# The zero-point column sums of an attention product: made once for the second half and added by VectorE, in place of two small products per tile and half row

## The chip, the cores and the metric

The kernel runs on one core of a Trainium2 chip. Times are device microseconds of one execution. The kernel before takes 328.64 us, the median of three runs (328.39 to 329.71).

## What is computed

The input x is [2, 512, 1024] in f32, so 1024 tokens in two halves (the two batches). Each half has its own context matrix of 1024 x 1024. Cut to what matters:

```
fake_quant(x) = (clip(round(x / s + z), 0, 255) - z) * s
x = x + tanh(g_xattn) * matmul(fake_quant(layernorm(x)), fake_quant(ctx))
h = layernorm(x)
x = x + tanh(g_ffn) * ( sum over 2 of 16 experts of gate * mlp_e(h)  +  mlp_shared(h) )
```

The quantized values are whole numbers. The kernel keeps them as f16 after taking 128 off (q - 128), so the matrix product of the stored values lacks terms in the difference between 128 and the zero point: one that depends on the output's row alone (row sums, `r1`), and one that depends on its column alone, (128 - z1) times the column sum of the stored context. The second is what the change is about.

## The kernel before, in words

Tokens lie in eight tiles of 128 (`NT` = 8), four per half (`TB` = 4). X holds them all in SBUF. The program is written per engine, with semaphores between them; each engine works through its own list in order.

- **Attention product.** For a tile i, `products(i, k)` makes two products of 128x512 for each of eight k (L1083), 16 in all, into two PSUM banks given by `AT_BANK` (tile 4: banks 0 and 1, tile 5: 2 and 3, tile 6: 4 and 5, tile 7: 6 and 7). `column_sums(i)` (L1086 to L1092) adds four more into the same banks: the stationary C1 holds (128 - z1) in each place, as a high and a low f16 half, and the moving S2 is the sum of the eight context blocks, so that each row of the result gets the scaled column sum. It then signals `at_done`.
- **Attend** (L711, VectorE) reads the two banks, scales them by `cf[:, 4:5]` and adds them to X. Then `bn` (L640 to L643) takes the statistics for the layer norm, GpSimd raises the variance to -0.5 (L373), `coefs` (L650, L651) gives scale and offset, and ScalarE writes the normed rows twice, in f32 and f16 (L433, L437). `ln2_lo` (L720, VectorE) makes the low f16 half, one tile behind. For the second half a DMA transpose on SyncE's queue (L275) then turns the tile.
- **Second half.** VectorE's list is, for i = 4 to 7 (L937 to L943): attend(i), bn(i), ln2_lo(i-1) from i = 5 on, coefs(i); then ln2_lo(7), and after it the four `sd_evac` (L742), and `route`. ScalarE's list is `hi_chunk("sw3", 0..3)` (L426), `ln_rows(4..7)`, then `add_r1` (L448), which signals `x_r1` for each tile, and the exponential of the router.
- **TensorE's list**: the shared up projection of the first half (L1145), row sums (L1103), the loop over tiles 4 to 7 (L1245 to L1256), and then `shared_down(i)` for the first half's tiles, 24 products each (L1184), into banks `SD_BANK` = (0, 2, 4, 0). Tile 0 waits for attend of tile 4, tile 1 for that of tile 5, tile 2 for that of tile 6. Tile 3 uses banks 0 and 1 again and waits for `sd_read` 1 (L1263), VectorE's first `sd_evac`. Behind it stand the router (L1191, L1193), which waits for the transposed tiles, the shared up projection of the second half, and then the experts (L1306, L1327).
- `su_gate` (L725, VectorE) signals `su_hf`; its fourth frees banks 6 and 7, in which the shared up projection had its last chunk. `clamp_ctx` (L677, L681) makes the context blocks and S2, and signals `s2_rdy`. `lo_chunk` is L694, `add_shared_bias` L956, `row_terms` L698.

Of the kernel before, what the change touches and what calls it, by code (L numbers as in the profile page):

```python
# [4 lines left out]
F32, F16, I32, I16 = mybir.dt.float32, mybir.dt.float16, mybir.dt.int32, mybir.dt.int16  # L5
ALU = mybir.AluOpType
ACT = mybir.ActivationFunctionType
AX = mybir.AxisListType.X

P = 128  # L10
B, S, D = 2, 512, 1024
KC = D // P
NT = B * S // P
TB = NT // B
# [3 lines left out]
SC = SI // P  # L18
# [15 lines left out]
def build(nc, x, ctx_in, g_xattn, g_ffn, x1_scale, x1_zp, x2_scale, x2_zp, router_w, router_b, router_bias,  # L34
# [5 lines left out]
    with es:  # L40
        def sb(name, shape, dt):
            return es.enter_context(nc.sbuf_tensor(name, shape, dt))
# [3 lines left out]
        def sem(name):  # L46
            sems[name] = es.enter_context(nc.semaphore(name))
            return sems[name]


        X = sb("X", [P, NT, D], F32)
# [11 lines left out]
        def view(area, lo, n, dt, pat=None, **kw):  # L63
            v = area[:, lo:lo + n]
            if dt is not F32:
                v = v.bitcast(dt)
            return v.rearrange(pat, **kw) if pat else v

        XT = view(areaT, 0, 8192, F16, "p (h k t) -> p h k t", h=2, k=KC)
        Q2 = view(area2, 0, 4096, F16, "p (k n) -> p k n", k=KC)  # L70
        Q1T = view(areaQ, 0, 2048, F16, "p (j k t) -> p j k t", j=TB, k=KC)
# [13 lines left out]
        S2 = sb("S2", [P, D], F16)  # L85
# [2 lines left out]
        ebr = sb("ebr", [E, SI], F32)  # L88
        EBT = sb("EBT", [P, 2 * HC, E], F32)
        GTE = sb("GTE", [P, NT, E], F32)  # L90
        gcol = sb("gcol", [P, 2, NT], F32)
        gcb = sb("gcb", [P, 2, NT], F32)
        ecol = sb("ecol", [P, 2, 2 * HC], F32)
# [7 lines left out]
        cf = sb("cf", [P, 16], F32)  # L101
# [10 lines left out]
        onesh = sb("onesh", [P, P], F16)  # L112
# [5 lines left out]
        PS = es.enter_context(nc.psum_tensor("PS", [P, 8, 512], F32))  # L118
# [31 lines left out]
        AT_BANK = (0, 4, 6, 2, 0, 2, 4, 6)  # L150
# [19 lines left out]
        c_int, q2_rdy, s2_rdy, c1_rdy = sem("c_int"), sem("q2_rdy"), sem("s2_rdy"), sem("c1_rdy")  # L170
# [3 lines left out]
        sbr_in, sb_T, sbT_rdy = sem("sbr_in"), sem("sb_T"), sem("sbT_rdy")  # L174
        r1_done = sem("r1_done")
        at_done, at_read = sem("at_done"), sem("at_read")
        ln_xs, ln_hi, ln_lo = sem("ln_xs"), sem("ln_hi"), sem("ln_lo")
        tk_T, tk_hi, tk_lo = sem("tk_T"), sem("tk_hi"), sem("tk_lo")
        rw_hi, rw_lo, sb3_in, b3_in, x_add = sem("rw_hi"), sem("rw_lo"), sem("sb3_in"), [sem("b3_in0"), sem("b3_in1")], sem("x_add")
        eb_in, eb_T, ebt_rdy = sem("eb_in"), sem("eb_T"), sem("ebt_rdy")  # L180
        su_done, su_silu, su_hf, su_hi, su_lo = sem("su_done"), sem("su_silu"), sem("su_hf"), sem("su_hi"), sem("su_lo")
# [20 lines left out]
        def arrived(eng, r):  # L202

            eng.wait_ge(ring_in[r % 4], 16 * (r // 4 + 1))
# [19 lines left out]
        def expert_count(eng):  # L224
            return eng.value_load(nact[0:1, 0:1], min_val=MIN_EXPERTS, max_val=E)
# [162 lines left out]
        def _(act):  # L388
# [30 lines left out]
            def hi_chunk(kind, k):  # L419
                r = RING_AT[kind, 0, k]  # L420
                arrived(act, r)
                if kind == "sw":
                    dst = SW[:, 0, k, :, :].rearrange("p k n -> p (k n)")
                else:
                    dst = SW3[:, 0, k, :]
                nc.scalar.activation(dst, ring[:, r % 4, :], ACT.Copy, scale=WS).then_inc(sw_hi, 1)  # L426

            def ln_rows(i):

                act.wait_ge(coef2, i + 1)  # L430
                if i >= 2:
                    act.wait_ge(ln_lo, i - 1)
                nc.scalar.activation(rows[:, i % 2, :], X[:, i, :], ACT.Identity, bias=lnB[:, i:i + 1],  # L433
                                     scale=lnA[:, i:i + 1]).then_inc(ln_xs, 1)
                if i >= TB + 2:
                    act.wait_ge(sw_lo, SW3_LO + SC)
                nc.scalar.activation(WROW[i][:, 0:D], X[:, i, :], ACT.Identity, bias=lnB[:, i:i + 1],  # L437
                                     scale=lnA[:, i:i + 1]).then_inc(ln_hi, 1)
# [78 lines left out]
            su_hi_of(3)  # L517
            hi_chunk("sw3", 2)
            hi_chunk("sw3", 3)
            for i in range(TB, NT):  # L520
                ln_rows(i)
            add_r1(0)
# [7 lines left out]
            def columns(a, j):  # L530

                e = expert_of(act, a)
                if not (isinstance(a, int) and a < 2):
                    act.wait_ge(y_rdy, NV * a - NV)
                    act.sem_inc(waited, 1)
                nc.scalar.activation(gcol[:, j, :], GTE[:, :, bass.ds(e, 1)].rearrange("p t o -> p (t o)"), ACT.Copy)\
                    .then_inc(cols_rdy, 1)
                nc.scalar.activation(gcb[:, j, :], GTE[:, :, bass.ds(e, 1)].rearrange("p t o -> p (t o)"), ACT.Copy,
                                     scale=DNS).then_inc(cols_rdy, 1)
# [60 lines left out]
            n = expert_count(act)  # L600
# [25 lines left out]
        def _(dve):  # L626
            chain = [0]

            def link(ins):

                chain[0] += 1
                ins.then_inc(v_chain, 1)
                dve.wait_ge(v_chain, chain[0])

            v = nc.vector
            norms = [0]

            def bn(i):
                for h in range(2):
                    ins = v.bn_stats(stats[:, i, 6 * h:6 * h + 6], X[:, i, h * 512:(h + 1) * 512])  # L640
                link(ins)
                link(v.bn_aggr(mv[:, i, :], stats[:, i, :]))
                v.tensor_scalar(lnV[:, i:i + 1], mv[:, i, 1:2], EPS, None, ALU.add).then_inc(mv_rdy, 1)  # L643
# [43 lines left out]
            def lo_chunk(kind, k):  # L687
                r = RING_AT[kind, 0, k]
                dve.wait_ge(sw_hi, (k if kind == "sw" else 2 * SC + k) + 1)
                if kind == "sw":  # L690
                    lo, hi = (SW[:, h, k, :, :].rearrange("p k n -> p (k n)") for h in (1, 0))
                else:
                    lo, hi = SW3[:, 1, k, :], SW3[:, 0, k, :]
                v.scalar_tensor_tensor(lo, ring[:, r % 4, :], WS, hi, ALU.mult, ALU.subtract).then_inc(sw_lo, 1)  # L694

            def row_terms(b):
                dve.wait_ge(r1_done, b + 1)
                v.tensor_scalar(r1[:, b * TB:(b + 1) * TB], PS[:, 3, 0:TB], cf[:, 7:8], cf[:, 6:7], ALU.mult, ALU.add)\  # L698
                    .then_inc(r1_rdy, 1)
# [7 lines left out]
            def attend(i):  # L707

                dve.wait_ge(at_done, i + 1)
                pb = AT_BANK[i]  # L710
                v.scalar_tensor_tensor(X[:, i, :].rearrange("p (h n) -> p h n", h=2), PS[:, pb:pb + 2, :], cf[:, 4:5],  # L711
                                       X[:, i, :].rearrange("p (h n) -> p h n", h=2), ALU.mult, ALU.add)\
                    .then_inc(at_read, 1)
                dve.wait_ge(at_read, i + 1)
# [57 lines left out]
            def route():  # L772
# [33 lines left out]
                link(v.tensor_tensor(t2, sco, t1, ALU.mult))  # L806
                v.tensor_scalar(GTE[:, :, :], t2, cf[:, 11:12], None, ALU.mult).then_inc(gte_rdy, 1)

# [61 lines left out]
            clamp_ctx(0, 6)  # L870
            link(v.tensor_scalar(cf[:, 9:10], sc6[:, 3:4], -1.0, HALF, ALU.mult, ALU.add))
            link(v.tensor_scalar(cf[:, 7:8], cf[:, 4:5], cf[:, 9:10], None, ALU.mult))
            link(v.tensor_scalar(cf[:, 6:7], cf[:, 7:8], cf[:, 8:9], float(D), ALU.mult, ALU.mult))
            row_terms(0)
            shared_biases()
# [58 lines left out]
            su_low(3)  # L934
            for c in range(1, SC):
                lo_chunk("sw3", c)
            for i in range(TB, NT):  # L937
                attend(i)
                bn(i)
                if i > TB:  # L940
                    ln2_lo(i - 1)
                coefs(i, 1, None, XS, None)
# [85 lines left out]
            n = expert_count(dve)  # L1028
# [35 lines left out]
        def _(pe):  # L1064
            mm = nc.tensor.matmul
# [14 lines left out]

            def products(i, k):
                for h in range(2):
                    mm(PS[:, AT_BANK[i] + h, :], Q1T[:, i % TB, k, :], Q2[:, k, h * 512:(h + 1) * 512],  # L1083
                       start=(k == 0), stop=False)

            def column_sums(i):  # L1086

                for h in range(2):
                    for n in range(2):
                        last = mm(PS[:, AT_BANK[i] + h, :], C1[:, n, :], S2[:, h * 512:(h + 1) * 512], start=False,  # L1090
                                  stop=(n == 1))
                last.then_inc(at_done, 1)  # L1092
# [112 lines left out]
            for k in range(2):  # L1205
                products(1, k)
# [34 lines left out]
            expert_bias_columns()  # L1241
            row_sums(1)
            pe.wait_ge(q2_rdy, 2 * KC)
            pe.wait_ge(s2_rdy, 2)
            for i in range(TB, NT):  # L1245
                if i == TB:
                    pe.wait_ge(tk_hi, TB)
                    pe.wait_ge(tk_lo, TB)
                if i == TB + 1:
                    pe.wait_ge(r1_rdy, B)  # L1250
                    pe.wait_ge(ebt_rdy, 2)
                if i >= TB + 2:
                    pe.wait_ge(su_hf, i - TB + 1)
                for k in range(KC):
                    products(i, k)
                column_sums(i)  # L1256

            pe.wait_ge(sw_lo, SW3_LO + SC)
            for i in range(TB):
# [31 lines left out]
            n = expert_count(pe)  # L1291
# [83 lines left out]
```

## Time and profile before

| | us |
|---|---|
| median of three runs | 328.64 |
| profiled execution, its own time | 328.81 |
| its span, first to last instruction | 327.0 |
| TensorE busy | 301.6 (92%) |
| VectorE busy | 196.6 (60%) |
| ScalarE busy | 113.6 (35%) |
| GpSimd busy | 15.1 (5%) |

In the profile PE is TensorE's matmuls, PEld its weight loads, DVE is VectorE, ACT is ScalarE, POOL is GpSimd and SP is SyncE. The chain is followed back from the last instruction, at each step to what released it. A timeline row can merge neighbours of one kind; a start that lies before the end of the row above is a pipelined instruction. What is idle before an instruction and who ended it stands in brackets behind it. Row ends of matmuls are modelled, so the distance between starts is the better measure.

### The profile page before, as it was taken

What the parts mean: (1) busy time and instruction counts of PE and PEld (TensorE: products, weight loads), DVE (VectorE), ACT (ScalarE), POOL (GpSimd) and SP (SyncE); (2) the same over time, 40 slices, a digit from 0 to 9 for tenths busy, and PEclk for the clock granted to TensorE, in tenths of its full rate; (3) what the DMA queues carried; (4) which work ended last, traced back from release to release, by engine and by line L of the source; (5) the groups of instructions that cost most, each with busy time, mean ns of one, the idle gap of its engine ahead of it and who ended that gap; (6) DMA issues with size and microseconds to landing.
All of it is one profiled execution on the core that took longest, in us unless ns stands there. A gap on an engine that the chain in (4) does not pass through costs nothing.

```text
span 327.0 us, 4761 instructions
## 1 busy us (share of the span) xinstructions
PE 301.6 (92%) x1895; PEld 153.7 (47%) x1895; DVE 196.6 (60%) x334; ACT 113.6 (35%) x128; POOL 15.1 (5%) x25
## 2 busy tenths in 40 slices
PE   0389879989999999999999999999999999999992
PEld 0234379964454444644444444444444444444441
DVE  3876995786698864585754445448744407125543
ACT  2887257867682369100113600127010001110000
POOL 2100210020000310000000000000000000000000
PEclk9999979999999999999999999999999999999998
DMA  7999044129980363000840003900000000000355
GB/s 268 416 317 299 1 130 130 43 95 222 310 299 1 69 125 64 2 2 0 274 176 3 0 0 112 335 4 2 0 1 0 2 0 0 3 0 0 129 206 186
DMA packets 32775, 34.56 MB, mean 106 GB/s; under 512 B 14788, under 2 KB 27116, under 8 KB 32748
## 3 DMA queue, kind: packets, MB, share of 16 engines
q1 hardware_dynamic: 32736, 34.20, 33.1%
q8 instruction: 17, 0.28, 0.4%
q14 instruction: 10, 0.08, 0.1%
q10 hardware_dynamic: 12, 0.00, 0.0%
HBM read 26.86 MB, written 4.19 MB: 95 GB/s over the span
## 4 chain that ended last, share of the span: by engine, by line
PE 82%; SPq 7%; DVE 5%; ACT 1%; DMA 1%; issue 1%; POOL 1%; DVEq 0%
PE PS L1306 25%; PE PS L1145 19%; PE PS L1327 13%; PE PS L1184 13%; PE PS L1083 5%; SPq L244 4%; PE PS L1161 3%; DVE stats L640 2%; SPq L236 1%; PE PS L1090 1%; DMA sbr<-in_L_ffn_sb_dram 1%; DVE X L711 1%; PE PS L1191 1%; DVE areaW L694 1%; PE PS L1169 1%
## 5 line engine op out<-in xcount | busy, mean ns | idle before, releaser
L1145 PE MATMUL PS<-areaT,areaW 128*128 128x512 f16 x288 | 62.6, 379 | 1.4 <-DVE SA L725 1.4
L1145 PEld LDWEIGHTS PS<-areaT,areaW 128*128 128x128 f16 x288 | 28.0, 98 | 35.0 <-DVE SA L725 1.6
L1184 PE MATMUL PS<-SW,areaH 128*128 128x512 f16 x192 | 41.8, 379 | 0.0
L1327 PE MATMUL PS<-areaW,areaH 128*128 128x512 f16 x192 | 41.8, 379 | 0.0
L1306 PE MATMUL PS<-areaT,area 128*128 128x512 f16 x192 | 41.6, 379 | 0.0
L1306 PE MATMUL PS<-areaT,areaW 128*128 128x512 f16 x192 | 41.6, 379 | 0.0
L584 ACT ACTIVATE SA<-PS,ecol 128x512 f32<-128x512 f32 x8 | 5.5, 687 | 93.2 <-PE PS L1306 93.2
L1083 PE MATMUL PS<-area,areaQ 128*128 128x512 f16 x128 | 31.2, 395 | 0.2
L1021 DVE SCALAR_TENSOR_TENSOR X<-PS,gcol,X 128x1024 f32<-128x1024 f32 (+1 forms) x18 | 21.0, 1164 | 15.8 <-PE PS L1327 15.8
L1327 PEld LDWEIGHTS PS<-areaW,areaH 128*128 128x128 f16 x192 | 18.8, 98 | 22.6
L1306 PEld LDWEIGHTS PS<-areaT,area 128*128 128x128 f16 x192 | 18.8, 98 | 22.7
L1306 PEld LDWEIGHTS PS<-areaT,areaW 128*128 128x128 f16 x192 | 18.8, 98 | 22.7
L1184 PEld LDWEIGHTS PS<-SW,areaH 128*128 128x128 f16 x192 | 18.8, 98 | 22.7
L992 DVE SCALAR_TENSOR_TENSOR SA<-PS,ecol,SA 128x512 f32<-128x512 f32 x8 | 6.0, 751 | 38.2 <-ACT SA L584 38.2
L640 DVE BATCH_NORM_STATS2 stats<-X 128x6 f32<-128x512 f32 x32 | 20.5, 682 | 4.3 <-DMA X<-in_x_dram 4.1
L1083 PEld LDWEIGHTS PS<-area,areaQ 128*128 128x128 f16 x128 | 12.4, 101 | 15.4 <-DVE area L677 1.3
L1009 DVE SCALAR_TENSOR_TENSOR X<-rows,gcb,X 128x1024 f32<-128x1024 f32 x16 | 19.5, 1279 | 0.0
L373 POOL TENSOR_TENSOR lnR<-lnV,mhalf 128x1 f32<-128x1 f32 (+1 forms) x13 | 13.5, 1035 | 102.3 <-DVE lnV L643 102.3
L1161 PE MATMUL PS<-areaT,areaW 128*128 128x128 f16 x256 | 16.6, 230 | 1.2 <-issue 1.2
L462 ACT ACTIVATE SA<-PS,sbT 128x512 f32<-128x512 f32 x8 | 5.5, 683 | 34.3 <-PE PS L1145 32.1
L433 ACT ACTIVATE rows<-X,lnB,lnA 128x1024 f32<-128x1024 f32 x8 | 9.9, 1240 | 20.7 <-DVE lnB L651 20.7
L1161 PEld LDWEIGHTS PS<-areaT,areaW 128*128 128x128 f16 x256 | 16.0, 104 | 1.4 <-issue 1.3
(152 smaller groups left out, 294.9 us busy)
## 6 DMA issues: line engine op xcount, KB each, us to landing
ring<-in_L_ffn_sw_dram SPq DMA_DIRECT2D x12, 512.0 KB, 5.1
X<-in_x_dram SPq DMA_DIRECT2D x8, 512.0 KB, 6.1
areaT<-in_ctx_dram SPq DMA_DIRECT2D x8, 512.0 KB, 10.9
ring<-in_ctx_dram SPq DMA_DIRECT2D x8, 512.0 KB, 3.8
ring<-in_L_ffn_ew_dram SPq DMA_DIRECT2D x4, 1024.0 KB, 7.7
out_dram<-X SPq DMA_DIRECT2D x7, 512.0 KB, 2.7
wrow<-in_L_ffn_ew_dram SPq DMA_DIRECT2D x2, 1024.0 KB, 9.8
rows<-in_L_ffn_eb_dram SPq DMA_DIRECT2D x2, 512.0 KB, 9.8
```

The source lines that it names most:

```text
L244: sp.dma_start(ring[:, r % 4, :].rearrange("p (k n) -> p k n", k=KC), w.rearrange("(k p) n -> p k n", p=P)[:, :, (k // 2) * P:(k // 2 + 1) ...
L373: nc.gpsimd.tensor_tensor(lnR[:, lo:lo + n], lnV[:, lo:lo + n], mhalf[:, 0:n], ALU.pow)\
L433: nc.scalar.activation(rows[:, i % 2, :], X[:, i, :], ACT.Identity, bias=lnB[:, i:i + 1], scale=lnA[:, i:i + 1]).then_inc(ln_xs, 1)
L640: ins = v.bn_stats(stats[:, i, 6 * h:6 * h + 6], X[:, i, h * 512:(h + 1) * 512])
L1009: v.scalar_tensor_tensor(X[:, i, :], rows[:, j, :], gcb[:, j, i:i + 1], X[:, i, :], ALU.mult, ALU.add)\
L1021: v.scalar_tensor_tensor(Xi, PS[:, pb + lo:pb + hi, :], gcol[:, j, i:i + 1], Xi, ALU.mult, ALU.add)\
L1083: mm(PS[:, AT_BANK[i] + h, :], Q1T[:, i % TB, k, :], Q2[:, k, h * 512:(h + 1) * 512], start=(k == 0), stop=False)
L1145: last = mm(PS[:, 4 + 2 * (c % 2) + w, lo:hi], SW[:, wp, 2 * c + w, k, :], XT[:, xp, k, tk], start=(k == 0 and n == 0), stop=(k == KC - 1 ...
L1161: mm(PS[:, 4 + 2 * c + w, tk], SW[:, 0, 2 * c + w, k, :], XT[:, xp, k, tk], start=(k == 0 and xp == 0), stop=False)
L1184: last = mm(PS[:, pb + h, :], HT[:, hp, c, i * P:(i + 1) * P], SW3[:, wp, c, hs], start=(c == 0 and n == 0), stop=(c == SC - 1 and n == 2))
L1306: last = mm(PS[:, 4 + 2 * (u % 2) + w, :], W12S[j][:, wp, w, k, c * P:(c + 1) * P], XT[:, xp, k, tk], start=(k == 0 and n == 0), stop=(k = ...
L1327: last = mm(PS[:, 2 * (i % 2) + h, :], HE[:, hp, c, i * P:(i + 1) * P], W3S[j][:, wp, c, hs], start=(c == 0 and n == 0), stop=(c == HC - 1 ...
```

## The change

For the second half alone, the column sums are made once. After the products of tile 4, TensorE multiplies a matrix of ones with S2, in two products, into banks 6 and 7, which tile 7 uses later (`column_row`, which waits for S2 and for the banks). It signals `cs_done`. ScalarE, after its last sw3 chunk and before its first layer norm row, reads the two banks, scales them by `cf[:, 5:6]` = `cf[:, 4:5]` x (128 - z1), and writes them to a new SBUF tile RC of 128x1024 f32 (`rc_rdy`). VectorE adds RC to each tile's X after attend and before the statistics, in f32 (`add_columns`). The `column_sums` of tiles 4 to 7, 16 products, are gone, and `at_done` comes from the last of the products. TensorE waits for `rc_rdy` before tile 7. The wait for `s2_rdy` 2 moves from ahead of tile 4 to `column_row`. The first half is as it was.

```diff
--- before.py
+++ after.py
@@ -88,6 +88,7 @@
         ebr = sb("ebr", [E, SI], F32)
         EBT = sb("EBT", [P, 2 * HC, E], F32)
         GTE = sb("GTE", [P, NT, E], F32)
+        RC = sb("RC", [P, D], F32)
         gcol = sb("gcol", [P, 2, NT], F32)
         gcb = sb("gcb", [P, 2, NT], F32)
         ecol = sb("ecol", [P, 2, 2 * HC], F32)
@@ -174,6 +175,7 @@
         sbr_in, sb_T, sbT_rdy = sem("sbr_in"), sem("sb_T"), sem("sbT_rdy")
         r1_done = sem("r1_done")
         at_done, at_read = sem("at_done"), sem("at_read")
+        cs_done, rc_rdy = sem("cs_done"), sem("rc_rdy")
         ln_xs, ln_hi, ln_lo = sem("ln_xs"), sem("ln_hi"), sem("ln_lo")
         tk_T, tk_hi, tk_lo = sem("tk_T"), sem("tk_hi"), sem("tk_lo")
         rw_hi, rw_lo, sb3_in, b3_in, x_add = sem("rw_hi"), sem("rw_lo"), sem("sb3_in"), [sem("b3_in0"), sem("b3_in1")], sem("x_add")
@@ -517,6 +519,9 @@
             su_hi_of(3)
             hi_chunk("sw3", 2)
             hi_chunk("sw3", 3)
+            act.wait_ge(cs_done, 1)
+            nc.scalar.activation(RC.rearrange("p (h n) -> p h n", h=2), PS[:, AT_BANK[NT - 1]:AT_BANK[NT - 1] + 2, :],
+                                 ACT.Identity, scale=cf[:, 5:6]).then_inc(rc_rdy, 1)
             for i in range(TB, NT):
                 ln_rows(i)
             add_r1(0)
@@ -870,6 +875,7 @@
             clamp_ctx(0, 6)
             link(v.tensor_scalar(cf[:, 9:10], sc6[:, 3:4], -1.0, HALF, ALU.mult, ALU.add))
             link(v.tensor_scalar(cf[:, 7:8], cf[:, 4:5], cf[:, 9:10], None, ALU.mult))
+            link(v.tensor_scalar(cf[:, 5:6], cf[:, 4:5], cf[:, 8:9], None, ALU.mult))
             link(v.tensor_scalar(cf[:, 6:7], cf[:, 7:8], cf[:, 8:9], float(D), ALU.mult, ALU.mult))
             row_terms(0)
             shared_biases()
@@ -934,8 +940,14 @@
             su_low(3)
             for c in range(1, SC):
                 lo_chunk("sw3", c)
+            def add_columns(i):
+
+                dve.wait_ge(rc_rdy, 1)
+                link(v.tensor_tensor(X[:, i, :], X[:, i, :], RC[:, :], ALU.add))
+
             for i in range(TB, NT):
                 attend(i)
+                add_columns(i)
                 bn(i)
                 if i > TB:
                     ln2_lo(i - 1)
@@ -1080,8 +1092,17 @@
 
             def products(i, k):
                 for h in range(2):
-                    mm(PS[:, AT_BANK[i] + h, :], Q1T[:, i % TB, k, :], Q2[:, k, h * 512:(h + 1) * 512],
-                       start=(k == 0), stop=False)
+                    last = mm(PS[:, AT_BANK[i] + h, :], Q1T[:, i % TB, k, :], Q2[:, k, h * 512:(h + 1) * 512],
+                              start=(k == 0), stop=(i >= TB and k == KC - 1))
+                return last
+
+            def column_row():
+
+                pe.wait_ge(s2_rdy, 2)
+                pe.wait_ge(su_hf, SC)
+                for h in range(2):
+                    last = mm(PS[:, AT_BANK[NT - 1] + h, :], onesh[:, :], S2[:, h * 512:(h + 1) * 512], start=True, stop=True)
+                last.then_inc(cs_done, 1)
 
             def column_sums(i):
 
@@ -1241,7 +1262,6 @@
             expert_bias_columns()
             row_sums(1)
             pe.wait_ge(q2_rdy, 2 * KC)
-            pe.wait_ge(s2_rdy, 2)
             for i in range(TB, NT):
                 if i == TB:
                     pe.wait_ge(tk_hi, TB)
@@ -1251,9 +1271,13 @@
                     pe.wait_ge(ebt_rdy, 2)
                 if i >= TB + 2:
                     pe.wait_ge(su_hf, i - TB + 1)
+                if i == NT - 1:
+                    pe.wait_ge(rc_rdy, 1)
                 for k in range(KC):
-                    products(i, k)
-                column_sums(i)
+                    last = products(i, k)
+                last.then_inc(at_done, 1)
+                if i == TB:
+                    column_row()
 
             pe.wait_ge(sw_lo, SW3_LO + SC)
             for i in range(TB):
```

## Rows read from the trace of the kernel before

**Rows 1.** The page: busy time by engine, and the chain that ended last.

```profile
PE 301.6 (92%) x1895; PEld 153.7 (47%) x1895; DVE 196.6 (60%) x334; ACT 113.6 (35%) x128; POOL 15.1 (5%) x25
...
PE 82%; SPq 7%; DVE 5%; ACT 1%; DMA 1%; issue 1%; POOL 1%; DVEq 0%
```

**Rows 2.** The chain in order of time, 93 to 132 us: start, length, what.

```profile
93.50 3.48 PE PS L1083 x16
96.97 0.86 PE PS L1090 x4
97.84 3.45 PE PS L1083 x16
...
110.79 20.72 PE PS L1184 x96
```

**Rows 3.** The chain in order of time, its last stages.

```profile
300.53 20.73 PE PS L1327 x96
```

**Rows 4.** Busy time by stretch: PE, PEld, DVE, ACT, POOL, granted clock, DMA share.

```profile
93.50:110.79 17.29, 17.29 (x81) 7.83 (x80) 15.82 (x28) 8.27 (x9) 2.05 (x2) 1.00 0.30 96
```

**Rows 5.** Timeline of VectorE, 92 to 125 us: start, length, instruction, idle before.

```profile
92.32 0.69 DVE L681 TENSOR_TENSOR S<-S,area 128x1024 f16<-128x1024 f16 x1
...
94.13 0.74 DVE L725 SCALAR_TENSOR_TENSOR SA<-PS,sbT,SA 128x512 f32<-128x512 f32 x1
...
99.94 1.27 DVE L711 SCALAR_TENSOR_TENSOR X<-PS,cf,X 128x1024 f32<-128x1024 f32 x1
101.24 1.29 DVE L640 BATCH_NORM_STATS2 stats<-X 128x6 f32<-128x512 f32 x2
...
103.90 1.28 DVE L711 SCALAR_TENSOR_TENSOR X<-PS,cf,X 128x1024 f32<-128x1024 f32 x1
...
108.79 1.28 DVE L711 SCALAR_TENSOR_TENSOR X<-PS,cf,X 128x1024 f32<-128x1024 f32 x1
...
113.68 1.28 DVE L711 SCALAR_TENSOR_TENSOR X<-PS,cf,X 128x1024 f32<-128x1024 f32 x1
...
121.16 1.23 DVE L720 TENSOR_TENSOR ring<-rows,ring 128x1024 f16<-128x1024 f32 x1 [2.51 <-ACT ring L437]
122.30 2.47 DVE L742 SCALAR_TENSOR_TENSOR X<-PS,cf,X 128x1024 f32<-128x1024 f32 x2
```

**Rows 6.** Timeline of ScalarE, 96 to 130 us.

```profile
96.86 1.06 ACT L426 ACTIVATE SW<-ring 128x1024 f16<-128x1024 f32 x1 [0.37 <-DMA ring<-in_L_ffn_sw_dram]
104.02 1.24 ACT L433 ACTIVATE rows<-X,lnB,lnA 128x1024 f32<-128x1024 f32 x1 [6.10 <-DVE lnB L651]
...
120.97 8.40 ACT L448 ACTIVATE X<-X,r 128x1024 f32<-128x1024 f32 x8
```

**Rows 7.** Timeline of VectorE around the early coefficients.

```profile
29.80 0.28 DVE L698 TENSOR_SCALAR r<-PS,cf 128x4 f32<-128x4 f32 x1 [1.18 <-PE PS L1103]
```

**Rows 8.** One line's instructions, L956: min, median and max of their ns.

```profile
L956 DVE SCALAR_TENSOR_TENSOR X<-areaQ,cf,X x8: 1279/1279/1281, 158.3 to 172.2; 128x1024 f32<-128x1024 f32 x8
```

**Rows 9.** One line's instructions, L275, on SyncE's queue, and their time to landing.

```profile
L275 SPq DMA_TRANSPOSE areaT<-ring x2: 1530/1738/1946, 117.9 to 122.5; - x2
...
DMA to landing us min/median/max: 4.2/4.3/5.9
```

**Rows 10.** Timeline of TensorE at 40 us, then the chain in order of time.

```profile
40.28 0.62 PE L1127 MATMUL PS<-idh,wrow 128*128 128x128 f16 x8 [1.07 <-ACT wrow L437]
...
43.55 5.36 PE PS L1161 x64
...
51.59 3.62 PE PS L1161 x64
```

**Rows 11.** Busy time by stretch, columns as in group 4.

```profile
44.30:47.70 3.40, 3.40 (x36) 3.40 (x34) 3.33 (x7) 1.41 (x2) 1.48 (x1) 0.51 0.54 159
```

**Rows 12.** Timeline of TensorE, the transposes of the first tiles.

```profile
14.26 1.03 PE L1078 MATMUL PS<-idh,areaQ 128*128 128x128 f16 x8 [2.42 <-DVE areaQ L665]
...
19.41 1.03 PE L1078 MATMUL PS<-idh,areaQ 128*128 128x128 f16 x8 [0.44 <-DVE areaQ L665]
```

## The prediction

> **What bounds the kernel now.** I read first the chain of work that ended last and the busy shares [rows 1]. TensorE is busy 92% of the span and holds 82% of the chain, so this is a TensorE kernel, and the first question is whether it waits anywhere near the change. The chain in order of time [rows 2] shows that it does not: from 93.50 us the pieces on TensorE follow one another without a gap, through the second half's attention, the 96 products of the shared down projection (20.72 us, so 5.18 for each of its four tiles, to 131.51) and on to the router. The stages behind it are chained on TensorE as well, up to the last product of the span at 321.26 [rows 3]. So whatever moves TensorE between 93 and 134 us moves the end by as much, as long as the others keep up.
>
> Then I asked who could fail to keep up. From 93.50 to 110.79 us VectorE is busy 15.82 of 17.29 us [rows 4], nearly as full as TensorE, and the change gives it more. Its queue in order of time [rows 5] shows one repeating unit per token tile: attend (L711), statistics (L640 to L643), a round trip to GpSimd, which the low half of the tile before (L720) nearly fills, and the coefficients. Attend starts at 99.94, 103.90, 108.79 and 113.68 us: a period of 4.89 us, made by VectorE and the round trip, not by the products, which end every 4.31 us [rows 2] and had run ahead. VectorE therefore already falls behind TensorE in this stage. After the fourth tile comes the wait for ScalarE's layer norm rows (2.51 us), then L720, then the first of the two L742 at 122.30, which frees banks 0 and 1 about 123.58. For that TensorE waits by `sd_read` before the fourth tile of the down projection, which it starts at 110.79 + 3 x 5.18 = 126.33. The slack is 126.33 - 123.58 = 2.75 us. This number decides the case.
>
> **The change part by part.** *Removed from TensorE:* 16 column products, 0.86 us for each four [rows 2], 3.44 us. *Added:* two products of the same shape, 2 x 0.215 = 0.43. Net 14 products, 3.01 us less work, all on the chain. The two have new waits. `su_hf` 4 is given by the L725 that starts at 94.13 and takes 0.74; `s2_rdy` 2 by the L681 of 92.32 [rows 5]. Both are past when the products of the first tile end at 96.97, so the waits cost nothing; with a VectorE 2 us later there they would begin to.
>
> *Added to ScalarE:* one Identity of 128x1024 out of PSUM. No row has this form. The nearest are 1.06 us for L426 and 1.24 for L433, both of that size and from SBUF [rows 6]; I take 1.24. ScalarE ends its last sw3 chunk at 97.92 and is then idle 6.10 us [rows 6]; the sums are there by 97.4 (96.97 + 0.43). So the row RC is ready about 99.1 and costs nothing there. Its two readers come later: VectorE at 101.24, TensorE's fourth tile (banks 6 and 7) at 93.50 + 3 x 3.45 + 0.43 = 104.3.
>
> *Added to VectorE, early:* one 128x1 link, an estimate of 0.2 us, just before the 1.18 us of idle time ahead of L698 [rows 7]. It is covered, and would cost its 0.2 us without that cover.
>
> *Added to VectorE, late:* four f32 additions of 128x1024 in SBUF, each between attend and the statistics of its tile, each waited for by the engine itself, with the statistics, GpSimd's power, the coefficients, ScalarE's two rows, the DMA transpose and the next attend queued behind it. The trace has no f32 addition of two f32 tensors. From below: L681 adds f16 tensors of this size in 0.69 us [rows 5]. From above: L956, f32 with a scalar, takes 1.279 [rows 8]. In between, and nearest in kind, L720 with one f32 operand takes 1.225 [rows 5]. I take 1.225, plus 0.03 us for the self-wait as between L711 at 99.94 (1.27 long) and L640 at 101.24: 1.25 us a tile. Nothing in the unit can absorb it: the addition is serial with the round trip, and every wait of the unit lies behind it. Four tiles give 5.0 us. (The Trainium skill, "VectorE: DVE Perf Modes", section "The perf-mode tier table", says that a `tensor_tensor` on fp32 has only the single rate and the doubled rate is for 16-bit; by that rule the four cost 4 x 1.25, by the f16 row 4 x 0.72. No row here shows the form itself.)
>
> *What is late then.* VectorE's start into the stage doesn't move: at 99.94 it comes from L694 work, not from the products. So the first L742 ends at 123.58 + 5.0 = 128.6 us. ScalarE's `x_r1` comes from L448, which follows the last L437 and moves from 120.97 to 126.0, with its first at 127.1 [rows 6]: just in time. TensorE arrives at the fourth tile at 126.33 - 3.01 = 123.3 and stands until 128.6, that is 5.3 us idle. Against 126.33 that is +2.3 us: the whole 3.0 is lost, and 2.3 more. The other waits of the down projection hold: tile 1 needs the second attend (105.2 + 1.25 = 106.4, against 113.0) and tile 2 the third (110.1 + 2.5 = 112.6, against 118.1). The last transposed tile lands about 122.5 + 4.2 + 5.0 = 131.7 [rows 9], and the router starts at 128.6 + 5.2 = 133.8 or later, so it stays hidden, by 2 us.
>
> *The clock.* A stall of this length hasn't happened to a warm TensorE in this trace. The nearest is the stretch from 39.2 to 43.55 us, where the engine, 1.07 us idle before L1127, did only small batches like the eight transposes of 0.62 us [rows 10]. 0.75 us after dense work had resumed, the granted clock fell to the lower level, 1.2 GHz, and stayed there 3.4 us [rows 11]. The 64 products that began at 43.55 took 5.36 us, the same 64 later 3.62 [rows 10]: 1.74 us lost. A stall of 5.3 us without any work should do it at least as surely. From above: at the start the eight transposes took 1.03 us at 14.26 and at 19.41 [rows 12], against 0.62 later [rows 10]. The slow rate thus lasted from 14.26 to about 20.4 (19.41 + 1.03) through mostly busy time, 6 us, of which half, 3.0, is lost. From below: zero. I take 2.1, near the one priced case and a little up, because here the idleness is complete. (The Trainium skill, "TensorE: Matmul & The Clock Gate", section "Part 1: The HAM clock gate", names the same two levels, 1.2 GHz after idleness and 2.4 after sustained work; by that the loss is there, without it the sum ends at +2.3.) No later wait covers this loss, as everything behind is chained on TensorE.
>
> **Sum.** -3.0 (products) + 5.3 (stall) + 2.1 (clock) = +4.4 us. The profiled execution is 328.81 us with a span of 327.0; the median of the runs is 328.64, 0.17 lower. So 333.2 against the profiled run, and 333.0 against the median.
>
> **The rivals.** (a) *Stall, but the clock holds.* For it: no row shows a fall after pure idleness of this length, and a stall that is shorter by a microsecond may pass. Against: less idleness than this was enough at 44 us. Time 328.64 + 2.3 = 330.9. (b) *The addition runs at the f16 rate.* Four times 0.72 is 2.9, so the release comes at 126.5, 0.1 after the old start: 328.8, and with a fallen clock up to 330.5. Against it stands L720, whose one f32 operand was enough for 1.225. (c) *The gain stays, faster.* If VectorE's delay never reached TensorE, because the order of waits left more slack than the profile shows or VectorE caught up, nearly all of the 3.0 would show: with the release still at 123.58 TensorE gains 2.75 us, 325.9. Every microsecond of delay to the first L742 comes straight off this gain, so that it decides from 2.75 us on, or 0.69 us a tile: an addition has to be cheaper than that. (d) *A long slow phase:* the lower clock lasts through the fourth tile and part of the router, 3.0 us or more: 333.9 to 334.6. (e) *The change doesn't do what it says*, with the two new products waiting: possible only if `su_hf` 4 came after 97.0, 2.1 us later than now; it would also give a slower kernel.
>
> **How the numbers follow.** The forecast (stall and a fallen clock, 331.9 to 333.8) has a chance of 0.62, (a) 0.16, (d) 0.08, (b) 0.06, (c) 0.07, (e) 0.01. The range 330.6 to 334.4 holds the forecast, (a) and most of (d). A difference under 0.5%, 1.6 us, can't be told from no change; (a) lies at +0.7%, close to it, so a part of it goes to "same": faster 0.08, same 0.10, slower 0.82.
>
> **What would show it.** In the profile after: 128 products of the shape of L1083 as before, but 2 in place of 16 column products in the second half; TensorE idle about 5.3 us before the fourth tile of the down projection, released by VectorE's evacuation; attend starts about 6.1 us apart instead of 4.89; the new addition x4 at about 1.22 us; a granted clock of 0.5 for some 3 to 5 us around 128 to 134 us. If the addition takes 0.7 us, (b) is true. If TensorE has no idle time there, my reading of the `sd_read` wait is wrong. If the clock stays at 1.00, (a) is true and I am 2 us too high. If ScalarE's row comes after 101.2 us, the delay is larger than my 5.0.

## The result: 1.3 to 1.5% slower

The changed kernel takes 332.88 us (median of six, 331.3 to 334.3), the kernel before 328.29 in the same group. The ratio is 1.0145, with a 95% interval of 1.0115 to 1.0176. A second group of the same two gave 332.83 us and 1.0128 (1.0093 to 1.0163). The prediction was 333.0. Two executions of the kernel with two additions, 331.39 and 814.59 us, count as slow and are left out of its median below.

The slices of the page before, for TensorE and its granted clock (each slice 8.2 us):

```profile
PE   0389879989999999999999999999999999999992
...
PEclk9999979999999999999999999999999999999998
```

The page of the profile after, its busy times and the same slices:

```profile
PE 300.1 (91%) x1881; PEld 151.3 (46%) x1881; DVE 201.6 (61%) x339; ACT 114.7 (35%) x129; POOL 15.1 (5%) x25
...
PE   0389789989999975999999999999999999999994
...
PEclk9999999999999996999999999999999999999998
```

TensorE has 14 matmuls fewer, VectorE 5.0 us more work. There is a hole in TensorE's line at slices 15 and 16, where there was none, and the clock of slice 16 is lower. The slice with a lower clock at 41 to 49 us is gone; that one comes and goes, as is shown below. The timeline of TensorE in this stretch (start, length, instruction, idle before), to be read against [rows 2]:

```profile
91.56 3.61 PE L1095 MATMUL PS<-area,areaQ 128*128 128x512 f16 x16
95.01 0.59 PE L1104 MATMUL PS<-S,onesh 128*128 128x512 f16 x2
95.44 10.52 PE L1095 MATMUL PS<-area,areaQ 128*128 128x512 f16 x48
105.80 15.70 PE L1205 MATMUL PS<-SW,areaH 128*128 128x512 f16 x72
126.96 8.21 PE L1205 MATMUL PS<-SW,areaH 128*128 128x512 f16 x24 [5.45 <-DVE X L747]
```

L1095 are the products that were L1083, L1104 the two new ones, L1205 the down projection that was L1184. The first three tiles of the down projection follow at once, the fourth stands 5.45 us until VectorE's evacuation (L747, before L742), and then takes 8.21 us, in place of the 5.34 that 24 products take in this view at the full clock (the kernel without additions, below). The busy time by stretch shows the same (PE, PEld, DVE, ACT, POOL, granted clock, DMA share, GB/s):

```profile
121.50:126.00 4.50, 0.01 (x1) 0.00 (x0) 1.92 (x4) 4.08 (x4) 0.00 (x1) 1.00 0.62 117
126.00:132.70 6.70, 5.74 (x14) 2.11 (x15) 3.20 (x3) 6.68 (x8) 0.00 (x0) 0.50 0.41 78
132.70:135.00 2.30, 2.30 (x11) 0.97 (x10) 0.00 (x0) 1.20 (x1) 0.00 (x0) 0.98 0.00 0
```

The granted clock is at its lower level, 1.2 GHz (0.50), from 126.0 to 132.7 us, after 4.5 us without work. VectorE's timeline, against [rows 5]:

```profile
98.13 1.28 DVE L716 SCALAR_TENSOR_TENSOR X<-PS,cf,X 128x1024 f32<-128x1024 f32 x1
99.44 1.23 DVE L946 TENSOR_TENSOR X<-X,RC 128x1024 f32<-128x1024 f32 x1
100.71 1.29 DVE L645 BATCH_NORM_STATS2 stats<-X 128x6 f32<-128x512 f32 x2
...
103.36 1.27 DVE L716 SCALAR_TENSOR_TENSOR X<-PS,cf,X 128x1024 f32<-128x1024 f32 x1
...
109.51 1.28 DVE L716 SCALAR_TENSOR_TENSOR X<-PS,cf,X 128x1024 f32<-128x1024 f32 x1
...
115.66 1.27 DVE L716 SCALAR_TENSOR_TENSOR X<-PS,cf,X 128x1024 f32<-128x1024 f32 x1
...
124.39 1.23 DVE L725 TENSOR_TENSOR ring<-rows,ring 128x1024 f16<-128x1024 f32 x1 [2.51 <-ACT ring L439]
125.53 3.66 DVE L747 SCALAR_TENSOR_TENSOR X<-PS,cf,X 128x1024 f32<-128x1024 f32 x3
```

The addition (L946) takes 1.23 us, attend (L716) comes 5.23 us after the first and then every 6.15 us, where it was 3.96 and then 4.89 [rows 5], and the first evacuation starts 27.40 us after the first attend (125.53 - 98.13). Before it was 22.36 (122.30 - 99.94). The delay is 5.04 us.

The books of the two profiled executions need the same view of TensorE before:

```profile
93.36 3.61 PE L1083 MATMUL PS<-area,areaQ 128*128 128x512 f16 x16
...
110.62 20.88 PE L1184 MATMUL PS<-SW,areaH 128*128 128x512 f16 x96
131.34 0.18 PE L1191 MATMUL PS<-RW,areaT 128*128 128x32 f16 x1
```

From the first products of the stage to the start of the router it was 131.34 - 93.36 = 37.98 us, and is 135.01 - 91.56 = 43.45 (the changed kernel's router begins at 135.01). The 5.47 us between them are -3.02 of products, +5.62 from where the fourth tile would have begun (105.80 + 15.54 = 121.34) to where it did (126.96), and +2.87 of slow clock in it (8.21 - 5.34). Yet the two times, 331.54 and 328.81, differ by 2.73 only. The stage began 1.8 us earlier, mostly because the kernel before happened to be profiled with a slow phase at 44 us [rows 10, 11] and the changed one without. The same 64 products as in [rows 10], in the timeline of the changed kernel:

```profile
42.98 3.73 PE L1182 MATMUL PS<-areaT,areaW 128*128 128x128 f16 x64 [1.16 <-issue]
```

That is 1.63 us less than 5.36. The rest (0.9 us) is behind the last product, in the last stores. It isn't the change's: from the start of VectorE's last instruction to the end of the span the profiled executions of these kernels take from 3.95 to 5.6 us: 5.5 in the kernel before, 4.5 in the changed one, 5.15 in the changed one run again. A single pair of profiles was therefore too kind to the change by about 2 us; the medians are not.

### The profile page after: what moved, and what is told of

Its sections match the earlier page's. It is cut to its first block, busy times and chain, and to the rows that moved or that the text cites. A ratio compares the mean times of both kernels' runs of the same rounds, so it can differ in the third digit from the quotient of the medians.

```text
span 329.7 us, 4744 instructions
## 1 busy us (share of the span) xinstructions
PE 300.1 (91%) x1881; PEld 151.3 (46%) x1881; DVE 201.6 (61%) x339; ACT 114.7 (35%) x129; POOL 15.1 (5%) x25
## 4 chain that ended last, share of the span: by engine, by line
PE 71%; DVE 17%; issue 3%; ACT 3%; POOL 2%; DMA 1%; ACTq 0%; POOLq 0%; DVEq 0%
PE PS L1330 25%; PE PS L1166 19%; PE PS L1351 13%; PE PS L1205 9%; DVE stats L645 4%; PE PS L1095 2%; DVE X L716 2%; POOL lnR L375 2%; DVE areaW L699 2%; DMA sc<-in_g_ffn_dram 1%; DVE X L946 1%; PE PS L1182 1%; DVE SW L699 1%; DVE mv L647 1%; DVE wrow L725 1%
## 5 line engine op out<-in xcount | busy, mean ns | idle before, releaser
L1205 PE MATMUL PS<-SW,areaH 128*128 128x512 f16 x192 | 44.8, 397 | 5.5 <-DVE X L747 5.5
L1166 PEld LDWEIGHTS PS<-areaT,areaW 128*128 128x128 f16 x288 | 28.0, 98 | 34.9 <-DVE SA L730 1.6
L1205 PEld LDWEIGHTS PS<-SW,areaH 128*128 128x128 f16 x192 | 19.4, 101 | 30.5 <-issue 9.7
L1095 PE MATMUL PS<-area,areaQ 128*128 128x512 f16 x128 | 30.9, 395 | 0.2
L1330 PEld LDWEIGHTS PS<-areaT,areaW 128*128 128x128 f16 x192 | 18.8, 98 | 22.6
L1095 PEld LDWEIGHTS PS<-area,areaQ 128*128 128x128 f16 x128 | 12.4, 100 | 15.4 <-DVE area L682 1.3
L1182 PE MATMUL PS<-areaT,areaW 128*128 128x128 f16 x256 | 14.9, 219 | 1.2 <-issue 1.2
L1182 PEld LDWEIGHTS PS<-areaT,areaW 128*128 128x128 f16 x256 | 14.4, 98 | 1.3 <-issue 1.3
```

Source lines behind the costliest of these rows:

```text
L1095: last = mm(PS[:, AT_BANK[i] + h, :], Q1T[:, i % TB, k, :], Q2[:, k, h * 512:(h + 1) * 512], start=(k == 0), stop=(i >= TB and k == KC - 1))
L1166: last = mm(PS[:, 4 + 2 * (c % 2) + w, lo:hi], SW[:, wp, 2 * c + w, k, :], XT[:, xp, k, tk], start=(k == 0 and n == 0), stop=(k == KC - 1 ...
L1182: mm(PS[:, 4 + 2 * c + w, tk], SW[:, 0, 2 * c + w, k, :], XT[:, xp, k, tk], start=(k == 0 and xp == 0), stop=False)
L1205: last = mm(PS[:, pb + h, :], HT[:, hp, c, i * P:(i + 1) * P], SW3[:, wp, c, hs], start=(c == 0 and n == 0), stop=(c == SC - 1 and n == 2))
L1330: last = mm(PS[:, 4 + 2 * (u % 2) + w, :], W12S[j][:, wp, w, k, c * P:(c + 1) * P], XT[:, xp, k, tk], start=(k == 0 and n == 0), stop=(k = ...
```

## The experiments

Each kernel was compared with the kernel before in its own group. Medians in us, and the ratio with its 95% interval:

| kernel | median | ratio |
|---|---|---|
| changed, again | 332.83 | 1.0128 (1.0093 to 1.0163) |
| changed, without additions | 325.62 | 0.9911 (0.9879 to 0.9943) |
| before, with additions | 332.61 | 1.0117 (1.0074 to 1.0160) |
| changed, stall filled | 330.24 | 1.0069 (1.0029 to 1.0108) |
| changed, two additions | 329.58 | 1.0045 (1.0012 to 1.0078) |
| changed, reordered | 325.19 | 0.9906 (0.9875 to 0.9938) |
| before, reordered | 328.82 | 1.0013 (0.9990 to 1.0037) |
| before, early pause filled | 327.36 | 0.9966 (0.9948 to 0.9984) |
| changed, reordered, early pause filled | 324.39 | 0.9890 (0.9855 to 0.9925) |
| changed, early pause filled | 331.80 | 1.0112 (1.0080 to 1.0144) |
| before, additions, early pause filled | 331.64 | 1.0093 (1.0058 to 1.0129) |
| changed, both filled | 330.29 | 1.0043 (1.0023 to 1.0063) |

### Are the additions the cause?

The changed kernel again:

> The changed kernel once more, as the reference of this group. Theory A (VectorE's four additions delay the release of banks 0 and 1, TensorE stands, and its clock falls for some microseconds in the stall): slower than the kernel before by 3 to 6 us, in two clusters about 2.7 us apart as in the first six executions (331.3 to 331.7 and 334.1 to 334.3), with a stall of about 5.4 us before the fourth tile of the down projection. Rival R (the difference comes from elsewhere, such as the longer stage before 93 us or ScalarE's new step): no stall of this kind, or one that varies with nothing else.

It came out at 332.83 us, from 331.6 to 334.2. Four of its six values (332.65 to 333.31) lie between the two clusters of the first six, so the two clusters that were expected did not come again. Its profile has the stall:

```profile
129.82 7.43 PE L1205 MATMUL PS<-SW,areaH 128*128 128x512 f16 x24 [5.46 <-DVE X L747]
```

Without the additions:

```diff
                 attend(i)
-                add_columns(i)
```

> The changed kernel with VectorE's four additions of RC left out (the second half lacks the zero-point column term); the two products, ScalarE's scaled row and every other wait stay. Theory A: the first evacuation ends where it ended before, TensorE waits 0.2 to 0.3 us there, attend comes every 4.9 us, and the kernel is 2.5 to 3.0 us faster than before, 325.5. Rival R (the two products' waits, ScalarE's step or the moved waits cost): still slower than before, or at best equal.

```profile
124.43 5.34 PE L1204 MATMUL PS<-SW,areaH 128*128 128x512 f16 x24 [0.42 <-DVE X L747]
```

325.62 us, a gain of 2.8. The fourth tile of the down projection waits 0.42 us (0.2 to 0.3 were expected). The two products, their waits and ScalarE's step cost nothing that can be seen; the saving is real, and all of the loss comes with VectorE's additions.

The other way round, the additions alone:

```diff
+            nc.gpsimd.memset(RC[:, :], 0.0).then_inc(rc_rdy, 1)
...
                 attend(i)
+                dve.wait_ge(rc_rdy, 1)
+                link(v.tensor_tensor(X[:, i, :], X[:, i, :], RC[:, :], ALU.add))
                 bn(i)
```

> The kernel before with only the four additions put in, of a tile of zeros that GpSimd writes early; all 16 column products stay. Theory A: attend comes every 6.1 us, VectorE's release is 5.0 us late against a slack of 2.75, so TensorE stands about 2.3 us before the fourth tile and the time is 2.3 us longer, 330.6, if the clock holds through so short a stall, and up to 2 us more if not. Rival R: within 0.5 us of before, as VectorE is busy only 60% of the span.

```profile
127.01 5.34 PE L1189 MATMUL PS<-SW,areaH 128*128 128x512 f16 x24 [2.44 <-DVE X L745]
```

A stall of 2.44 us where 2.3 were expected. The profiled execution took 329.51 us and the next 329.94, both with a mean granted clock of 1.000; the other four took 332.2 to 333.3, at 0.980 to 0.989. The median, 332.61, is at the upper end of what was expected, and equals that of the changed kernel. So the change has the same time as the additions alone: what the 14 products save is spent waiting.

Two of the four additions:

```diff
-                add_columns(i)
+                if i < TB + 2:
+                    add_columns(i)
```

> The changed kernel with the addition of RC for the first two tiles of the second half only (the other two lack the column term). Theory A is a threshold with a slope behind it: from the kernel without additions (-2.8 us against before, TensorE already waits 0.4 us) each addition adds its 1.25 us to the stall in full. Two additions: a stall of 2.9 us, and -2.8 + 2.5 = -0.3 us against before with the clock held, 328.2; up to 2 us more where it falls. Rival R2 (the cost comes from something that happens once, such as the first addition's wait for ScalarE's row): the time is already that of the changed kernel, 332.8.

```profile
124.94 5.34 PE L1206 MATMUL PS<-SW,areaH 128*128 128x512 f16 x24 [2.94 <-DVE X L747]
```

The stall is 2.94 us, as the slope of 1.25 an addition gives (0.42 + 2.5). The time is 329.58 us, 1.2 above before, in the upper part of the expectation. It isn't one value: the three executions whose mean clock was 0.998 or more took 326.4 to 327.3 us, the other seven 329.5 to 331.3. The profiled one is of the first kind: its clock was 1.000, and the tile behind a stall of 2.94 us took the full-speed 5.34 us. The slope is shown for the stall; in the time the clock covers it.

### What the clock costs

24 products without use where TensorE stands:

```diff
                 if i == 3:
+                    pe.wait_ge(at_read, NT)
+                    for _ in range(24):
+                        mm(PS[:, 6, :], HT[:, 0, 0, 0:P], SW3[:, 0, 0, 0:512], start=True, stop=True)
                     pe.wait_ge(sd_read, 1)
```

> The changed kernel with 24 products more, 5.2 us of TensorE work without any use, put where TensorE stands before the fourth tile (into bank 6, whose content has been read). Theory A with the clock: the products end just before the release, so they cost nothing, and the granted clock stays at its higher level there; the time falls to about 330.5 (before + 2.3), 1 to 3 us under the changed kernel, although there is more work. Rival (the slow phase has another cause, or there is no cost to it): equal to the changed kernel; or slower by up to 5 us if the stall was not idle time.

```profile
121.67 5.34 PE L1289 MATMUL PS<-SW,areaH 128*128 128x512 f16 x24
127.20 5.35 PE L1205 MATMUL PS<-SW,areaH 128*128 128x512 f16 x24 [0.19 <-DVE X L747]
```

330.24 us: more work, and 2.6 us faster than the changed kernel of the same group. The products fit into the stall, and the fourth tile behind them takes 5.35 us in place of 7.4 to 8.2. But its executions spread from 328.3 to 332.4, so something else varied too.

That was the pause at 39 to 43.5 us. Products without use there, in the kernel before, with the waits that they need (`at_read` 1 moves ahead of them, `sw_hi` 1 and `at_read` 2 are new):

```diff
+                if i == 0:
+                    pe.wait_ge(at_read, 1)
+                    pe.wait_ge(sw_hi, 1)
+                    keep_busy(4, 0)
                 pe.wait_ge(ln_hi, i + 1)
...
-                if i == 0:
-                    pe.wait_ge(at_read, 1)
...
+                if i == 0:
+                    keep_busy(3, 1)
                 pe.wait_ge(ln_lo, i + 1)
...
             transpose_tokens(0)
+            pe.wait_ge(at_read, 2)
+            keep_busy(5, 4)
```

> The kernel before with 12 products without any use, put where TensorE waits around its first token transposes at 39 to 43.5 us (4 before the first batch, 3 between the batches, 5 before the first blocks; 2.6 us in all). Theory C (the spread of a kernel's own executions, 326.9 to 330.4, comes from this pause: the granted clock after it fell in some executions and not in others, for 3.4 or 6.8 us): the clock stays up in all, the spread shrinks, and the median falls by 1 to 2 us to about 327. Rival: the spread and the median stay as they are, or the time rises by up to 1 us because the products delay the transposes.

327.36 us in twelve executions from 326.2 to 327.8, where the kernel before, run beside it, went from 325.8 to 330.1. The mean clock was 0.996 to 1.000 in all twelve. The same stretch in an execution whose clock fell, that of the changed kernel run again, and in this one:

```profile
41.80:48.70 6.90, 5.71 (x53) 5.47 (x54) 6.61 (x12) 3.50 (x4) 0.55 (x1) 0.51 0.52 153
```

```profile
38.00:43.00 5.00, 4.57 (x32) 2.04 (x30) 4.86 (x9) 3.82 (x5) 1.46 (x1) 1.00 0.33 101
43.00:50.00 7.00, 6.65 (x117) 6.50 (x117) 6.90 (x11) 4.94 (x5) 1.48 (x1) 1.00 0.41 112
```

The pause lets the clock fall for 3.4 us [rows 11], for 6.9, or not at all (the changed kernel's first profile). This is most of the spread between executions of the kernel before (4.3 us without these products, 1.6 with them), and it is now out of the way for the stall. Three more kernels have the 12 early products. The changed kernel with them:

> The changed kernel with the 12 early products, which take away the spread of the early stage, so that the cost of its stall stands alone. Theory A with the clock: against the kernel before with the same early products (327.4) the delay gives 2.4 us and the clock after 5.4 us of idle time 1.7 to 3.0 us in every execution: 331.5 to 332.8. Rival: if the clock loss in the changed kernel came mostly from the early pause, it is 327.4 + 2.4 = 329.8.

The additions alone with them:

> The kernel before with the four additions and the 12 early products: a stall of 2.4 us alone. With the clock held in all executions 327.4 + 2.4 = 329.8 in a narrow group. If a stall as short as this lets the clock fall in some, there are two groups, the other 1.3 to 3 us later; its share shows whether the additions alone, whose four of six executions were at 332 to 333, owe this to the stall or to the early pause.

The changed kernel with both pauses filled:

> The changed kernel with both sets of products without use: the 12 in the early pause and the 24 in the stall. Against the same kernel without the 24 (331.8) it differs in the clock after the stall alone. Theory A with the clock: the 24 cost nothing and the clock stays up in every execution, so the early kernel's 327.4 plus the 2.4 us of delay, 329.8 or a little under, in a group 1.5 us wide; the clock's share of the change's loss is then 2.0 us. Rival: if the clock's share is smaller than this and the group of 331.8 owes more to the stall, it stays above 331.

The changed kernel with the early pause filled takes 331.80 us (331.0 to 332.8), in the lower part of the range. None of its six executions had a mean clock above 0.990, though the early pause was filled, so by its mean clock each lost time behind the stall; in the profiled one the fourth tile took 7.46 us. Its stall is a little longer than that of the changed kernel:

```profile
127.95 7.46 PE L1213 MATMUL PS<-SW,areaH 128*128 128x512 f16 x24 [5.92 <-DVE X L747]
```

With the stall filled as well it takes 330.29 (328.7 to 330.9), 0.5 above what was expected: with the early products VectorE's release comes later against TensorE's stage by some tenths of a microsecond, and 0.56 us of waiting were left behind the 24 products. By the ratios the clock after the stall costs 1.0112 - 1.0043, that is 0.7% or 2.3 us, by the medians 1.5. The delay itself costs 1.0043 - 0.9966, 0.8% or 2.5 us, by the medians 2.9. These are differences between groups, and the intervals of the ratios leave each of them open by about 1 us either way. Both terms are clear of zero; how the loss divides between them is known no better than that.

The additions alone with the early pause filled surprised me. The clock did not hold in all executions:

```profile
127.56 7.03 PE L1197 MATMUL PS<-SW,areaH 128*128 128x512 f16 x24 [2.58 <-DVE X L745]
```

```profile
125.00:127.10 2.10, 0.00 (x0) 0.00 (x0) 2.10 (x2) 2.10 (x3) 0.00 (x0) 1.00 0.23 42
127.10:131.90 4.80, 4.34 (x13) 1.69 (x14) 2.70 (x3) 4.80 (x5) 0.00 (x0) 0.64 0.58 109
```

After a stall of 2.58 us the clock fell here, and the tile took 7.03 us; one execution of six had a mean clock of 1.000 and took 329.36 us, the other five took 330.4 to 332.4. So a stall of this length was enough in most executions, but not in all: it held behind the 2.44 us of the additions alone and the 2.94 us of the kernel with two additions, in the executions that were profiled. The five are 1.1 to 3.0 us above the one whose clock held; without the early products the four slower executions of the additions alone were 2.3 to 3.8 above the two whose clock held. So most of it is the stall's, the rest the early pause's.

### Can the saving be kept?

```diff
+            add_r1(0)
             for i in range(TB, NT):
                 ln_rows(i)
-            add_r1(0)
             add_r1(1)
...
-                if i > TB:
+                if TB < i < NT - 1:
                     ln2_lo(i - 1)
+                if i == NT - 1:
+                    sd_evac(0)
                 coefs(i, 1, None, XS, None)
+            ln2_lo(NT - 2)
             ln2_lo(NT - 1)
-            for i in range(TB):
+            for i in range(1, TB):
                 sd_evac(i)
```

> The changed kernel, all four additions kept, with three steps reordered: ScalarE's add_r1 of the first half goes ahead of its second-half layer norm rows, VectorE's first sd_evac takes the place of ln2_lo(6) beside the last round trip to GpSimd, and ln2_lo(6) moves into the 2.5 us in which VectorE waits for ScalarE. Theory A (only the late release of banks 0 and 1 hurts): the release comes about 6.8 us earlier, at the time TensorE arrives, no stall, and the 14 fewer products show: 325.4 to 326.0, as without additions. Rival R3 (VectorE's later end of the stage then stops TensorE at the router, whose last tile lands about when it is needed): a stall of 0.5 to 2 us there, 326 to 327.5. Rival R (additions cost by being on the chip): as the changed kernel.

325.19 us. The timelines of VectorE and TensorE:

```profile
121.49 1.28 DVE L747 SCALAR_TENSOR_TENSOR X<-PS,cf,X 128x1024 f32<-128x1024 f32 x1
122.69 0.14 DVE L655 TENSOR_SCALAR lnA<-lnR 128x1 f32<-128x1 f32 x1
...
125.54 1.22 DVE L725 TENSOR_TENSOR ring<-rows,ring 128x1024 f16<-128x1024 f32 x1 [1.36 <-ACT ring L439]
```

```profile
107.41 20.88 PE L1208 MATMUL PS<-SW,areaH 128*128 128x512 f16 x96
131.58 8.79 PE L1169 MATMUL PS<-areaT,areaW 128*128 128x512 f16 x40
```

The evacuation now ends at 122.77, just before TensorE asks for it (107.41 + 15.54 = 122.95), and the 96 products run through in 20.88 us. All four additions are still there. The stall at the router that rival R3 put at 0.5 to 2 us came to 0.2: before the last products of the router a weight load waits for the DMA transpose that feeds them.

```profile
PEld PS L1215 <- DMA areaT<-ring: 0.2, 1, 0.2
```

So in this execution the last tile lands just when it is needed, and there is no slack left to give away there.

> The kernel before with the same three reorderings and nothing else. Theory A: TensorE didn't wait for this release before, it had 2.75 us of slack, so nothing changes: 328.4, within 0.5 us. Rival: the reordering itself speeds something up, then it is faster here as well, and the gain of the reordered changed kernel isn't due to the column products.

The same order in the kernel before gives nothing, 1.0013 (0.9990 to 1.0037). The gain needs both the fewer products and the earlier release.

> The reordered changed kernel with the 12 products without use in the early pause. If the two effects are separate, their gains add: 325.2 - 1.0 = 324.2, and the executions lie within 1.6 us of one another. If the early products matter only through something the reordering changed as well, it stays at 325.2.

324.39 us, 1.1% under the kernel before: the two gains roughly add (324.2 was expected), though the executions lie 3.0 us apart, not 1.6. It is the fastest of these kernels and has the column term in full.

## Why the prediction was right, step by step

- **The products.** -3.01 us expected, -3.02 measured from the stage's first product to the down projection (17.26 us before, 14.24 after). Without additions 2.8 of it showed.
- **The new products' waits and ScalarE's row.** No wait; RC was ready at 96.98 us, 2.5 before its first reader. ScalarE's step took 1.10 us against my 1.24. The early 128x1 link took 0.21 us and was covered: 0.43 us of idle time were still left behind it, where [rows 7] had 1.18.
- **The addition.** 1.225 us expected by the row with one f32 operand, 1.224 measured. The rule of the Trainium skill ("VectorE: DVE Perf Modes", "The perf-mode tier table"), which keeps fp32 `tensor_tensor` at the single rate, agrees. Rival (b) is out.
- **The delay and the slack.** A delay of 5.0 us was expected against a slack of 2.75, and 5.04 measured: each of the four intervals up to the evacuation grew by about 1.26 us, the first, shorter one (3.96 us before, which my period of 4.89 passed over) like the others. The stall was 5.3 us expected, 5.45 measured (5.62 from start to start). The slack was confirmed from both sides, and measured: 0.42 us of waiting without additions make it 3.02 - 0.42 = 2.60 us, and 2.44 with the additions and the old products make it 5.04 - 2.44 = 2.60. With it the stall is 3.02 + 5.04 - 2.60 = 5.46.
- **The clock.** 2.1 us chosen between 0 and 3.0. The profile shows 2.87 for this execution and 2.09 for the next (7.43 - 5.34), the filled pair 1.5 to 2.3. The size was right. A clock that held was not seen in the changed kernel: none of its executions had a mean clock above 0.990, with the early pause filled or not. My upper bound rests on less than I thought: at the start, where the transposes took 1.03 us and products of 128x512 ran at about 0.48 us each, the view gives a granted clock of 1.00, so the slow rate there is read from lengths alone.

```profile
14.00:20.50 6.50, 5.66 (x24) 2.49 (x24) 4.92 (x15) 5.07 (x6) 0.81 (x1) 1.00 1.08 370
```

- **The closeness is partly luck.** The mechanism and its terms hold to a microsecond; 333.0 against 332.88 is closer than they are. In the profiled pair the stage lost 5.47 us where the sum has 4.4, and the difference of the medians is 4.6; the median before was 328.64 of three executions and is 328.29 of six.
- **What I had weak.** Rival (a) rested on the thought that a stall a microsecond shorter may pass. One of 2.4 to 2.6 us, half as long, mostly doesn't. And I took the slow phase at 44 us for a fixed part of the kernel before; it comes and goes, and most of the 4.3 us by which its executions differ is due to it. The median wasn't hurt, since both kernels have the pause.

## What to carry to other kernels

Work taken off the busiest engine is a gain only as far as its next releaser has slack. Read both times at the wait, and compare the work that goes to the releaser with the slack. More work than slack makes the kernel slower by the difference, whatever the busiest engine saves, and the saving shows in full only where the work is no more than the slack less the saving. Here 5.0 us met a slack of 2.75 (2.6 as measured) and a saving of 3.0, so the kernel had to lose, and even with no work added 0.4 us of the saving would have gone into waiting. Three steps moved in two queues made the release earlier and brought the whole saving back. In this kernel a stall of TensorE of 5.4 us cost about 2 us more for the clock behind it, and half that length cost it in most executions; price both, and don't judge a change of 1% from one pair of profiles.

## What the hardware showed that I had not expected

After a long stretch of dense products a stall of 2.58 us let the granted clock fall to 1.2 GHz in the profiled execution, and by their times and mean clocks in four of the five others; the 24 products behind it took 7.03 us in place of 5.34. In two other kernels, whose stalls were 2.44 and 2.94 us, the profiled executions kept the full clock, so the length of the stall alone doesn't decide it. The slow phase after the same pause in the code lasted 3.4 us in one execution, 6.9 in another, and was absent in a third. And 24 products without use, put into a stall of 5.4 us, made the kernel 1.5 to 2.6 us faster (by medians, with and without the early pause filled).
